# Layer 0's state scan with channel and state on the partitions, its operands spread by DMA

## The reference

```python
xr = x @ w_in                                  # x: attention output plus its input
u0, res = (xr[..., :D_INNER], xr[..., D_INNER:])
u = silu(causal depthwise conv of u0 over 4 steps + conv_b)
x_dbl = u @ w_xproj                            # 8 columns for the step, 16 for B, 16 for C
delta = softplus(x_dbl[..., :DT_RANK] @ w_dt + b_dt)
A = -exp(A_log)
def step(h, inp):                              # per batch, over 256 steps
    dA = exp(d_t[..., None] * A)
    h = dA * h + (d_t * u_t)[..., None] * b_t[:, None, :]
    y = einsum('bdn,bn->bd', h, c_t)
y = (ys + u * Dp) * silu(res)
return y @ w_out
```

## Time and profile before

| | us |
|---|---|
| median of 3 runs (2733.96 to 2741.33) | 2738.44 |
| profiled execution, its own time | 2741.92 |
| span of its instructions | 2740.6 |
| layer 0, to its last result | about 915 |
| TensorE busy in the span | 2382.2 (87%) |
| VectorE busy | 2008.0 (73%) |
| ScalarE busy | 1402.8 (51%) |
| GpSimd busy | 859.5 (31%) |

### The profile page before, as it was taken

One profiled execution on the slowest core, in us unless ns is written; L12 is line 12 of the kernel. 1 busy time (PEld: TensorE's weight loads), 2 busy tenths in 40 slices (PEclk: granted clock), 3 DMA queues, 4 the chain that ended last, 5 costly groups with the idle time before them and its releaser, 6 DMA issues.

```text
span 2740.6 us, 47437 instructions
## 1 busy us (share of the span) xinstructions
PE 2382.2 (87%) x18265; PEld 1723.4 (63%) x18265; DVE 2008.0 (73%) x4327; ACT 1402.8 (51%) x3576; POOL 859.5 (31%) x459
## 2 busy tenths in 40 slices
PE   4799999999997879999999999779999976888886
PEld 2467777776765746666666666545565555666665
DVE  3489999899988527777777777646666625888887
ACT  1365555555554127767776767423444333545453
POOL 0045445444455102333332333200000002555553
PEclk9899999999998969999999999979999998989888
DMA  2011111111112720000000000001100003445453
GB/s 67 17 42 38 49 47 48 40 40 48 48 48 85 238 85 1 1 1 1 1 2 1 1 1 1 22 5 31 31 21 8 7 25 124 145 167 173 163 180 110
DMA packets 71346, 148.16 MB, mean 54 GB/s; under 512 B 6864, under 2 KB 37072, under 8 KB 70608
## 3 DMA queue, kind: packets, MB, share of 16 engines
q1 hardware_dynamic: 69072, 140.93, 15.6%
q0 software_dynamic: 2048, 4.20, 0.4%
HBM read 135.40 MB, written 9.18 MB: 53 GB/s over the span
## 4 chain that ended last, share of the span: by engine, by line
PE 41%; DVE 14%; ACT 11%; issue 4%; POOL 1%; DMA 0%; POOLq 0%; DVEq 0%; ACTq 0%; SPq 0%
PE psum L566 3%; ACT pr L1865 3%; PE psum L486 3%; ACT dA L1817 3%; PE psum L320 2%; PE psum L397 2%; PE psum L611 2%; PE psum L675 2%; PE psum L424 2%; PE psum L679 2%; PE psum L727 2%; PE psum L402 2%; PE psum L580 2%; DVE h L1301 2%; DVE h L1310 2%
## 5 line engine op out<-in xcount | busy, mean ns | idle before, releaser
L2111 POOL TENSOR_TENSOR h<-h,Crep 128x1024 f32<-128x1024 f32 x128 | 365.1, 2862 | 541.5 <-DVE h L1520 541.5
L2093 POOL TENSOR_TENSOR pr<-pr,rsum 128x512 f32<-128x512 f32 x192 | 234.9, 1230 | 550.2 <-DVE rsum L1376 550.2
L1410 DVE TENSOR_REDUCE mx<-psum 128x4 f32<-128x1024 f32 (+1 forms) x192 | 229.9, 1214 | 111.4 <-PE psum L684 111.4
L1520 DVE TENSOR_TENSOR_SCAN h<-dA,h 128x1024 f32<-128x1024 f32 x128 | 293.1, 2310 | 2.5
L1909 ACT ACTIVATE pt<-psum 128x1024 f32<-128x1024 f32 x192 | 188.9, 1020 | 170.7 <-PE psum L686 170.3
L856 PE MATMUL psum<-h,pack_wf 128*128 128x256 f32 x1024 | 245.4, 394 | 7.2 <-POOL h L2111 7.2
L2145 POOL TENSOR_TENSOR h<-h,Crep 128x1024 f32<-128x1024 f32 x64 | 179.7, 2807 | 219.7 <-DVE h L1301 219.5
L2006 ACT ACTIVATE dA<-delta,A 128x255 f32<-128x255 f32 x512 | 213.3, 498 | 31.6 <-DVE h L1520 30.5
L856 PEld LDWEIGHTS psum<-h,pack_wf 128*128 128x128 f32 x1024 | 199.0, 199 | 40.0 <-POOL h L2111 10.2
L1865 ACT ACTIVATE pr<-psum,nb 128x256 f32<-128x256 f32 (+1 forms) x512 | 210.0, 428 | 16.6 <-DVE nb L1368 15.8
L1875 ACT ACTIVATE prT<-psum 128x512 f32<-128x512 f32 x192 | 115.9, 604 | 150.2 <-PE psum L580 148.1
(11 more groups left out here) (337 smaller groups left out, 5188.7 us busy)
## 6 DMA issues: line engine op xcount, KB each, us to landing
Crep<-c_rows SPq DMA_DIRECT2D x64, 512.0 KB, 3.9
Brep<-bc_rows SPq DMA_DIRECT2D x64, 512.0 KB, 6.7
Crep<-bc_rows SPq DMA_DIRECT2D x64, 512.0 KB, 6.0
w1r<-m_w SPq DMA_DIRECT2D x32, 256.0 KB, 6.4
w2r<-m_w SPq DMA_DIRECT2D x32, 256.0 KB, 6.4
pack_wf<-wf SPq DMA_DIRECT2D x1, 3192.0 KB, 10.4
slots<-zero SPq DMA_DIRECT2D x12, 256.0 KB, 6.9
w1s<-s_w SPq DMA_DIRECT2D x8, 256.0 KB, 2.8
```

The costliest lines, as they stand in the source:

```text
L1410: ve.e.tensor_reduce(mx[:, qb, 2 * h:2 * h + 2, groups[0]:groups[-1] + 1], k.psum[:, base:base + 2, :].rearrange("p i (n x) -> p i n x", n ...
L1520: ve.e.tensor_tensor_scan(flat(h), flat(k.dA[c][g % 2]), flat(h), 0.0, ALU.mult, ALU.add).then_inc(*k.set("scanned", 0, b, g, c))
L2093: po.e.tensor_tensor(p3, p3, bcast(k.rsum[n][:, 0:len(heads[r])], P * (q + 1), 2), ALU.mult).then_inc(*k.set("normed", 1, b, p, r))
L2111: po.e.tensor_tensor(h[:, :, :], h[:, :, :], k.Crep[n % 3][:, :, :], ALU.mult).then_inc(*k.set("hC", 0, b, g, c))
```

## The change

State tiles of layer 0 now carry 8 channels x 16 states on the 128 partitions and four channel groups of 256 steps along the row, again 128 x 1024 and again 8 a batch. Channel c*128 + 32*s + 8*j + m sits in tile n = 8b + 4c + j, row stretch s. `delta` and `dtu` are written to memory by 8 DMAs each (32 partitions x 1 KB) and read back by one DMA of 512 KB for each tile: `delta` into one of 5 `dA` tiles, where ACT takes the exponential in place, and `dtu` into one of 6 `h` tiles, where DVE multiplies it in place with B. B is the same for all tiles of a batch, so one pair of matmuls writes it for all 128 partitions into bank 6, where it stays for the batch. C is made likewise and copied once to SBUF by ACT. The sums over states become matmuls with a 128 x 32 selecting matrix (`pick`), one for each of the four column groups of the array. The step's two projections are merged into one weight matrix (`w_step`) at the start. The gate half of `w_in` goes to bank 5, so `u` no longer needs the `zc` step. `selb`, the splits and the dA column memsets go; 512 KB of zeros are written to `delta_rows` once, while loading. The order tables of layer 0 are new, and SP has one too.

```diff
-SPREAD_BANK, Y_BANK = 6, 7
+B_BANK, Y_BANK = 6, 7
+NH, NDA, AHEAD = 6, 5, 2
...
+        "pe_inner": (11, 18, 19, 23, 32),
+        "pe_out": (1, 3, 7, 12, 15),
+        "pe_pre0": (2, 8, 9, 13, 20, 21, 26, 34),
+        "pe_results": (14, 16),
+        "pe_states": (29, 30),
+        "pe_summing": (5, 6, 22, 24, 31),
+        "pe_wide0": (0, 4, 10, 17, 25, 27, 28, 33, 35, 36),
+        "ve_inner": (1, 38, 40, 42),
+        "ve_out": (7, 8, 10, 16, 18, 22),
+        "ve_pre0": (3, 5, 6, 12, 15, 17, 24, 26, 27, 30, 32, 33, 35, 46, 51),
+        "ve_results": (0, 14, 20, 28),
+        "ve_states": (2, 4, 19, 21, 23, 25, 31, 34, 36, 37, 41, 43, 44, 45, 49, 50, 52),
+        "ve_wide0": (9, 11, 13, 29, 39, 47, 48),
+        "ac_inner": (14, 15, 17, 19, 25),
+        "ac_out": (0, 10),
+        "ac_pre0": (1, 4, 5, 6, 8, 11),
+        "ac_states": (3, 7, 13, 16, 18, 22, 23, 24, 29),
+        "ac_wide0": (2, 9, 12, 20, 21, 26, 27, 28, 30, 31),
+        "sp_reads": (0, 1, 2, 3, 4, 5, 6, 7, 8, 9, 10, 12, 13, 17, 18, 19, 20),
+        "sp_store": (11, 14, 16),
+        "sp_turned": (15, 21),
...
-    pe, w, bo, x1T = k.pe, k.w, k.bank[OUT_BANK[0]], k.x1T[b % 3]
+    pe, w, bo, x1T, u = k.pe, k.w, k.bank[OUT_BANK[0]], k.x1T[b % 3], k.su[b % 2]
     yield
     pe.wait_ge(*k.at("x1T", b))
     for c in range(CI):
             i = pe.e.matmul(bo[:, c * L:(c + 1) * L], k.w_tap[:, j, c, :], x1T[:, j:j + L], start=j == 0, stop=j == CONV - 1)
     i.then_inc(*k.set("w_in", b, 0))
     yield
-    pe.wait_ge(*k.at("zc", b))
+    bk = pe_take(k, 0)
     for c in range(CI):
-        i = pe.e.matmul(bo[:, c * L:(c + 1) * L], w["w_in"][:, CI + c, :], x1T[:, CONV - 1:], start=True, stop=True)
+        i = pe.e.matmul(bk[:, c * L:(c + 1) * L], w["w_in"][:, CI + c, :], x1T[:, CONV - 1:], start=True, stop=True)
     i.then_inc(*k.set("w_in", b, 1))
-    yield
-    u = k.su[b % 2]
+    k.pre_read = ("res", b)
+    yield
     bk = pe_take(k, 0)
     pe.wait_ge(*k.at("u", b))
     for c in range(CI):
-        pe.e.matmul(bk[0:96, 0:L], w["w_bc"][:, c, :], u[:, c, :], start=c == 0, stop=c == CI - 1)
-    for c in range(CI):
-        i = pe.e.matmul(bk[0:DTR, L:2 * L], w["w_dtin"][:, c, :], u[:, c, :], start=c == 0, stop=c == CI - 1)
-    i.then_inc(*k.set("bc", 0, b))
-    k.pre_read = ("bc_read", b)
-    yield
-    bk = pe_take(k, 0)
-    for c in range(CI):
-        i = pe.e.matmul(bk[:, c * L:(c + 1) * L], w["w_dt"][:, c * P:(c + 1) * P], k.dtT[:, :], start=True, stop=True)
+        for m in range(CI):
+            i = pe.e.matmul(bk[:, c * L:(c + 1) * L], k.w_step[:, m, c * P:(c + 1) * P], u[:, m, :], start=m == 0, stop=m == CI - 1)
     i.then_inc(*k.set("dt", 0, b))
     k.pre_read = ("delta", 0, b)
-SPREADS = ((1, 1), (2, 0), (2, 1), (3, 0), (3, 1), (4, 0), (4, 1), (5, 0))
-def pe_spread(k, b, g, j):
-    pe, w, SB = k.pe, k.w, k.bank[SPREAD_BANK]
-    pe.wait_ge(*k.at("split", 0, b))
-    was = (b, g, 0) if j else (b, g - 1, 1) if g else (b - 1, 3, 1) if b else None
-    if was is not None:
-        pe.wait_ge(*k.at("dbu", 0, *was))
-    for m in range(2):
-        i = pe.e.matmul(SB[:, m * L:(m + 1) * L], w["sel"][:, g * NG + 2 * j + m, :], k.split[b % 2][:, :], start=True, stop=True)
-    i.then_inc(*k.set("spread", 0, b, g, "B", j))
+    yield
+    bk = pe_take(k, 0)
+    for m in range(CI):
+        i = pe.e.matmul(bk[:, 0:L], w["w_crep"][:, m, :], u[:, m, :], start=m == 0, stop=m == CI - 1)
+    i.then_inc(*k.set("crep", b))
+    k.pre_read = ("c_copied", b)
...
+def pe_states(k, b):
+    pe, w, x = k.pe, k.w, b + 1
+    yield
+    if x >= NB:
+        return
+    pe.wait_ge(*k.at("u", x))
+    if x:
+        pe.wait_ge(*k.at("dbu", 0, 8 * x - 1))
+    for m in range(CI):
+        i = pe.e.matmul(k.bank[B_BANK][:, 0:L], w["w_brep"][:, m, :], k.su[x % 2][:, m, :], start=m == 0, stop=m == CI - 1)
+    i.then_inc(*k.set("brep", x))
 def pe_sums(k, b, g):
     pe, w, YB = k.pe, k.w, k.bank[Y_BANK]
-    for c in range(CI):
-        h = k.h[c][g % 2]
-        pe.wait_ge(*k.at("hC", 0, b, g, c))
-        if g == 0 and c == 0 and b:
+    for x in (2 * g, 2 * g + 1):
+        n, c, j = 8 * b + x, x // 4, x % 4
+        pe.wait_ge(*k.at("hC", 0, n))
+        if x == 0 and b:
             pe.wait_ge(*k.at("y_read", b - 1))
-        for n in range(NG):
-            i = pe.e.matmul(YB[:, c * L:(c + 1) * L], w["ident"], h[:, n, :], start=g == 0 and n == 0 and c == 0,
-                            stop=g == 3 and n == NG - 1, skip_group_check=True)
-        i.then_inc(*k.set("summed", 0, b, g, c))
-def pe_states(k, b):
-    for g, j in SPREADS:
-        yield
-        if 0 <= b + g // 4 < NB:
-            pe_spread(k, b + g // 4, g % 4, j)
+        for s in range(4):
+            i = pe.e.matmul(YB[32 * s:32 * s + 32, c * L:(c + 1) * L], w["pick"][:, j, :], k.h[n % NH][:, s, :], start=j == 0,
+                            stop=j == 3, tile_position=(0, 32 * s), skip_group_check=True)
+        i.then_inc(*k.set("summed", 0, n))
...
+def ve_product(k, n):
+    ve, h = k.ve, k.h[n % NH]
+    ve.wait_ge(*k.at(f"h_in{n % NH}", 0, n))
+    ve.wait_ge(*k.at("brep", n // 8))
+    ve.e.tensor_tensor(h[:, :, :], h[:, :, :], bcast(k.bank[B_BANK][:, 0:L], 4, 1), ALU.mult).then_inc(*k.set("dbu", 0, n))
+def ve_scan(k, n):
+    ve, h = k.ve, k.h[n % NH]
+    ve.wait_ge(*k.at("dA", 0, n))
+    ve.wait_ge(*k.at("dbu", 0, n))
+    ve.e.tensor_tensor_scan(flat(h), flat(k.dA[n % NDA]), flat(h), 0.0, ALU.mult, ALU.add).then_inc(*k.set("scanned", 0, n))
...
+    ac.e.preload_act_table_set("silu_and_others")
     ac.wait_ge(*k.at("w_in", b, 0))
     if b >= 2:
         ac.wait_ge(*k.at("yT", b - 2))
-        ac.wait_ge(*k.at("bc", 0, b - 2))
+        ac.wait_ge(*k.at("crep", b - 2))
+        ac.wait_ge(*k.at("brep", b - 2))
     for c in range(CI):
-        i = ac.e.activation(su[:, c, :], bk[:, c * L:(c + 1) * L], ACT.Identity, bias=w["conv_b"][:, c:c + 1])
-    i.then_inc(*k.set("zc", b))
-    yield
-    ac.e.preload_act_table_set("silu_and_others")
-    ac.wait_ge(*k.at("zc", b))
-    ac.e.activation(su[:, 0:CI, :], su[:, 0:CI, :], ACT.Silu)
+        i = ac.e.activation(su[:, c, :], bo[:, c * L:(c + 1) * L], ACT.Silu, bias=w["conv_b"][:, c:c + 1])
+    i.then_inc(*k.set("u", b))
...
+    ac.wait_ge(*k.at("crep", b))
+    if b >= 2:
+        ac.wait_ge(*k.at("hC", 0, 8 * b - 9))
+    ac.e.activation(k.Crep[b % 2][:, :], bk[:, 0:L], ACT.Copy).then_inc(*k.set("c_copied", b))
...
+    for n in range(8 * b + 2, 8 * b + 10):
+        yield
+        if not 0 <= n < 8 * NB:
+            continue
+        ac.wait_ge(*k.at(f"dA_in{n % NDA}", 0, n))
+        dA = k.dA[n % NDA]
+        for s in range(4):
+            i = ac.e.activation(dA[:, s, 1:], dA[:, s, 1:], ACT.Exp, scale=k.A0[:, n % 8, s:s + 1])
+        i.then_inc(*k.set("dA", 0, n))
...
+    po.wait_ge(*k.at("c_copied", b))
+    for n in range(8 * b, 8 * b + 8):
+        h = k.h[n % NH]
+        po.wait_ge(*k.at("scanned", 0, n))
+        po.e.tensor_tensor(h[:, :, :], h[:, :, :], bcast(k.Crep[b % 2][:, :], 4, 1), ALU.mult).then_inc(*k.set("hC", 0, n))
...
+def sp_turned(k, b):
+    yield
+    if b + 1 < NB:
+        sp_negmax(k, 0, b + 1)
+def sp_store(k, b):
     sp = k.sp
-    sp.wait_ge(*k.at("crow", b))
+    yield
+    sp.wait_ge(*k.at("delta", 0, b))
     if b >= 2:
-        for n in range(4 * b - 8, 4 * b - 4):
-            sp.wait_ge(*k.at(f"c_spread{n % 3}", n // 4, n % 4))
-    sp.e.dma_start(k.c_rows[b % 2, :, :], k.crow[b % 2][NS:2 * NS, :]).then_inc(*k.set(f"c_stored{b % 2}", b, by=16))
+    stored_rows(k, 0, b, "delta", k.delta_rows, k.delta[b % 2], 1)
+    yield
+    sp.wait_ge(*k.at("dtu", b))
+    stored_rows(k, 0, b, "dtu", k.dtu_rows, k.dtu[b % 2], 0)
+def sp_reads(k, b):
+    sp = k.sp
+    for n in range(8 * b + AHEAD, 8 * b + 8 + AHEAD):
+        x, c, j = n // 8, n % 8 // 4, n % 4
+        yield
+        if 0 <= n < 8 * NB:
+            sp.wait_ge(*k.at(f"delta_stored{x % 2}", 0, x))
+            if n >= NDA:
+                sp.wait_ge(*k.at("scanned", 0, n - NDA))
+            sp.e.dma_start(flat(k.dA[n % NDA]), read_rows(k, k.delta_rows, x, c, j)).then_inc(*k.set(f"dA_in{n % NDA}", 0, n, by=16))
+        yield
+        if 0 <= n < 8 * NB:
+            sp.wait_ge(*k.at(f"dtu_stored{x % 2}", 0, x))
+            if n >= NH:
+                sp.wait_ge(*k.at("summed", 0, n - NH))
+            sp.e.dma_start(flat(k.h[n % NH]), read_rows(k, k.dtu_rows, x, c, j)).then_inc(*k.set(f"h_in{n % NH}", 0, n, by=16))
+def stored_rows(k, l, b, name, rows, src, first):
+    sp = k.sp
+    for s in range(4):
+        for c in range(rows.shape[1]):
+            sp.e.dma_start(rows[b % 2, c, :, s, first:], src[32 * s:32 * s + 32, c, first:]).then_inc(
+                *k.set(f"{name}_stored{b % 2}", l, b, by=16))
+def read_rows(k, rows, b, c, j):
+    return bcast(rows[b % 2, c, 8 * j:8 * j + 8, :, :].rearrange("m s t -> m (s t)"), NS, 1)
...
+    k.dA, k.h = k.two("dA", [P, 4, L], n=NDA), k.two("h", [P, 4, L], n=NH)
```

(15 more changed lines are left out.)

163 lines of the change are left out of this document (33 added, 130 removed).

## The result

| | before | after |
|---|---|---|
| median, same chip, 4 runs each | 2739.88 | 3077.4 (3069.22 to 3082.99) |
| ratio | | 1.1234, interval 1.1202 to 1.1266 |
| span of the profiled execution | 2740.6 | 3074.0 |

The account below looks back on a forecast made before the run. TensorE and VectorE both nearly full in layer 0, afterwards VectorE alone. Savings of 39 us (twelve turns), 7 (three short turns) and 6 (last stretch) total 52: 2741.9 to 2690, less 3.5 gives 2686 us; range 2650 to 2732.

Parts of the forecast that it names:

- 16 reads of 512 KB and the stores are 8.9 MB a turn, 23 us of transfer at that rate: Layer 0 memory traffic per turn (one `dtu` to the next): it fits, at the 381 GB/s layer 3 reached.
- The rival that came nearest: Memory sets layer 0's turn: late stores or reads make the product wait 4.5 us; 49.6 a turn, 2731 us; chance 0.14.
- VectorE's work, 44.8 us a turn: Layer 0: VectorE's work falls from 46.5 to 44.8 us (44.2 at best), and VectorE alone sets the turn.
- The six small operations: VectorE in layer 0: six small operations of the B path go, saving 1.9 us a turn.
- because a maximum now stands between: VectorE's waits in layer 0: 0.3 us a turn kept, for a maximum between `z_min` and `delta`.
- TensorE, about 37 us a turn: Layer 0: TensorE's work falls by 10.6 us a turn from 47.9, with four column groups running at once.
- Eight stores in 3.0 us, landed 1.4 later, `h`'s read issued 4.3 after `dtu`: SP's path through memory in layer 0: `dtu` stores land about 4.3 us after `dtu`, then the `h` read goes out.
- A read of 512 KB lands in 5.5 us: Layer 0's `h` read: 5.5 us, between 3.9 alone and 6.7 with several under way; 9.8 us after `dtu`.
- Tiles come back in time.: Layer 0's tile reuse: scan, POOL and sum take 6 us; VectorE is six tiles further only after more than 15.
- The clock rival: TensorE's clock falls through gaps in layer 0: a turn of 55 us if 18 us run cold, 2813 us; chance 0.08.
- Column groups one after another: Layer 0's new sums run one after the other: TensorE keeps 47 us a turn, 2725 us; chance 0.05.
- The forecast of 46.6 us a turn: Layer 0's turn falls from 49.86: 44.8 of VectorE work, 1.5 of memory waits, 0.3 of other waits; between 44.5 and 49.

Follow-up runs that it names:

- run 1: The changed kernel with state slow and channel fast in the partition order, so a read's source has 16 outermost, not 8: 2793.3 us, ratio 1.021.
- run 2: The changed kernel, still on 8 engines, with each `h` read fetching two of four row stretches, 256 KB instead of 512: 2745.56 us, one execution.
- run 12: The changed kernel with 8 `h` and 6 `dA` tiles in place of 6 and 5, nothing else: 3077.12 us, one execution.
- run 7: Run 1 with all 128 partitions reading the same 4 KB row, as layer 3's reads do: 2760.59 us, one execution.
- run 4: Run 1 with `z_min` written as an operation with two inputs: 2799.78 us, ratio 1.0224.
- run 5: Run 4 with channels in natural order in memory, `delta` and `dtu` stored by one DMA each instead of eight: 2731.11 us, ratio 0.998.
- run 6: Run 1 with the 4 KB rows in memory 5 KB apart: 2801.97 us, one execution.
- run 8: Run 5 with the one-input `z_min` and the step's projection ahead of the first group's sums: 2748.21 us, ratio 1.0044.
- run 9: Run 8 with reads four tiles ahead (`AHEAD` 4, not 2) and SyncE's order made to suit: 2770.14 us, ratio 1.0114.
- run 11: Run 8 with 8 `h` tiles in place of 6 and 6 `dA` tiles in place of 5: 2713.45 us, ratio 0.9907.
- run 3: The changed kernel without its 16 reads a turn: exponentials taken from `delta`, products from `dtu`, stores kept: 2702.3 us, one execution.

## Why the prediction was wrong

**The step that failed** is "16 reads of 512 KB and the stores are 8.9 MB a turn, 23 us of transfer at that rate". The bytes are right. The rate, 381 GB/s, was taken from layer 3, whose reads have another source pattern, and it was wrong twice. First, the source of the new reads has 8 as its outermost dimension, and 8 of 16 engines ran: 8.9 MB at 129 GB/s are 69 us, which is the turn of 68.7. Shown by the packets in flight (8 or 9, then 16 or more in run 1) and by runs 1, 2 and 12. Second, eight different rows are read at some 250 GB/s by 16 engines, not 381: run 7, worth 1.4 us a turn. None of the rows of before shows a 512 KB read with so small an outermost dimension, so they could not have shown the first; but I set no lower bound on the rate, which would have been the place for a rival. The Trainium skill (DMA: Bandwidth & Descriptors, Rules for kernel authors) has the rule: how many engines a DMA uses is set by the slowest dimension of its access patterns that is not 1, and one of size c under 16 keeps it to at most c engines. By it the share would be at most 8/16; the trace shows 0.50. I did not weigh it against `read_rows`, where the 8 stands in the diff; half of the 381 alone would have made the transfers 47 us a turn (an estimate), already more than VectorE's 44.8.

**The rival that came nearest**, memory setting the turn, had the right resource, the product as the place, and the wrong size: a wait of 4.5 us where after waits 182.1 us in 500, some 25 a turn. Its mechanism (stores late, SyncE's line behind them) is much of what runs 1 and 4 to 9 then show once the engines are 16: turns of 49.5 to 53.7 against its 49.6, and times of 2731 to 2802 against its 2731.

By the other steps, each measured where the rate does not cover it:

- **VectorE's work, 44.8 us a turn.** Run 11: 46.4 a turn less 21.4 us of waits in 8.6 turns, 2.5 each, is 43.9. Right within 1 us. (The 21.4 are seven rows, of which the first two are shown above.) The products take 1.215 us (forecast 1.28 in length, from the earlier trace rows); the earlier trace rows's maxima out of PSUM, 1.208, were the better neighbour. Scans stay at 2.28 to 2.31.
- **The six small operations.** They are gone, as said. But a seventh, `z_min`, now stands right behind the scan that releases GpSimd's product, and where it loses the race for the start it takes 2.57. The sum had no term for it: 2.2 us in most turns of runs 1 and 3, and nothing in after, where it is 0.40 or 0.41 in every turn but the first (0.43). The 0.3 "because a maximum now stands between" was put at the wrong operation.
- **TensorE, about 37 us a turn.** Run 3: 80.2% of 47.8 us is 38.3, at a mean clock of 0.93. Right within 4%. Four column groups do run at once; in after, 16 recorded sum matmuls take 1.07 us behind a stretch at clock 1.00, 0.067 each, against 0.216 in the earlier trace rows. Forecast 0.06:

```profile
535.63 1.07 PE L856 MATMUL psum<-h,pack_wf 128*32 128x256 f32 x16
```

- **Eight stores in 3.0 us, landed 1.4 later, `h`'s read issued 4.3 after `dtu`.** Wrong in each part. The issues take 3.56 and 4.44 us in after, they land after 3.1 and 2.9, and the read goes out 10.7 us after `dtu` there, 7.3 in run 1. The price was that of a small store alone in the queue, and the earlier trace rows. Run 5, with one store in place of eight, gained 4.2 us a turn, not all of it by the stores.

```profile
542.45 3.56 SPq L2176 DMA_DIRECT2D delta_rows<-delta  x8
546.05 4.44 SPq L2176 DMA_DIRECT2D dtu_rows<-dtu  x8
...
555.50 0.59 SPq L2168 DMA_DIRECT2D h<-dtu_rows  x1
```

- **A read of 512 KB lands in 5.5 us.** Wrong: by the pages `h`'s reads take 8.7 in run 1, over 16 engines, and 12.1 in run 11. The forecast had two under way; SyncE issues eight in a row in run 1 and ten in run 11.
- **"Tiles come back in time."** Not tested in after, where the rate hides it (SyncE stands 121.5 us of 500 at the sums there, and the DMA engines are busy all the same); wrong in run 8, where two more tiles took 2.6 us off the turn.
- **The clock rival.** The clock did fall, to 0.81 in 400:500 from 0.97, but beside a wait that was there for another reason: TensorE was idle a third of the time, and VectorE waited for DMA, not for it. In run 11 it is 1.00 there. **Column groups one after another:** excluded by the row above.

The forecast of 46.6 us a turn is near what the idea gives when its transfers are done well: run 11's trace has 46.4, and its layer 0 ends at 875.86 where it ended at 914.64, 38.8 us earlier. But this is its fastest execution, 12 us under its median; the medians of the whole kernel differ by 28, about half of the 52 forecast. That 46.4 is so close to 46.6 is in part luck: run 11 has one store in place of eight and a deeper ring, which the forecast kernel did not have, and its reads are slower than forecast.

## What to carry to other kernels

Price a new DMA by its own source pattern: take the outermost dimension of both sides, ask on how many of the 16 engines that can run, and borrow a rate only from a read with the same pattern; in a profile, a DMA share that stands at a plain fraction (0.50 here) while an engine waits for reads is a sign to look for this fault. Count the issues and landings of many small stores at the price they have in a row, not alone, and store in the order that makes it one DMA. A tile of a ring must be free before the read of its successor can be issued, so when one engine's order is changed, follow who frees what for the queue; and do not expect a gain from the ring's depth while the rate is the bound.

## What the runs showed of the hardware that I had not expected

- The rate of an engine depends on what is read. All 16 full, eight different 4 KB rows come at 229 to 258 GB/s in most stretches (14 to 16 GB/s an engine; after's eight engines 129 / 8 = 16, so it is not a limit on the total), one row for all partitions at 266 to 416. A distance of 5 KB between the rows changes nothing. In run 2, with 2 KB of each row, 98 GB/s at a share of 0.29 make 21 for an engine at work. Why is open.
- `z_min` takes 0.40 us where it starts 0.16 before GpSimd's product, and 2.56 where it starts 0.06 behind.
- An issue of a 512 KB read mostly costs SyncE 0.57 to 0.59 us with 8 engines and 0.52 to 0.60 with 16; 0.43 for `Crep` in the earlier trace rows. But in after, with seven reads issued just before, the next one takes far longer, while ten in a row in run 11 stay at 0.53 to 0.62 each. So with 8 engines the backlog reached SyncE itself (an inference from these rows):

```profile
506.13 0.57 SPq L2162 DMA_DIRECT2D dA<-delta_rows  x1
506.74 5.60 SPq L2168 DMA_DIRECT2D h<-dtu_rows  x1
```
